# Six layers of local attention and gated feed-forward on one core: a new order for the weight loads at a change of layer

## The chip, the cores and the metric

The kernel runs on one core of one Trainium2 chip. The metric is the device time of one execution in microseconds (us). An execution is one launch that computes the whole output from inputs in device memory.

## The reference, cut to what matters

The input x is 32 sequences of 128 tokens of 128 values. A cross attention of 16 small heads (4 key heads) is added to it, and the result x1 is normalized. Then six layers run, each with its own weights, and x1 is added to what comes out:

```python
def shift_tokens(t):                      # 2nd half of the features comes from the token before
    a, s = split(t, 2, -1); s = pad(s, one token in front)[:, :-1]
    return concatenate([a, s], -1)
for i in range(6):
    x = attn_layer(shift_tokens(x), Wqkv[i], q_scale[i], k_scale[i], Wo[i]) + x
    x = ffn_layer(shift_tokens(x), ln_g[i], ln_b[i], W1[i], b1[i], W2[i], b2[i]) + x
```

`attn_layer` computes q, k and v with one 128 x 3072 matrix (16 heads of 64), normalizes q and k, rotates them with a table, attends in windows of 32 tokens (each window sees itself and the one before), and multiplies by the 1024 x 128 matrix Wo. `ffn_layer` is a layer norm with scale and bias, a product with W1 (128 x 682), a * gelu(gate), and a product with W2 (341 x 128) plus b2. Everything is in float32.

## The kernel before, in words

**Units and slots.** A unit is one sequence in one layer, so there are 6 x 32 = 192 units; unit u belongs to layer u // 32. All engines run the same list of slots (`slots`, L241), and a slot n works on several units at once, each at another stage: unit n is projected to q, k and v, unit n-2 is transposed and its scores are made, unit n-3 attends, unit n-4 goes through Wo, the second token shift, the layer norm and the product with W1, and unit n-5 through W2. A unit so takes six slots. Slots 6 to 189 are in a loop with two slots in its body, in which semaphore targets are computed from the loop's register; the slots before and after it are written out with constants. There is one buffer for each of the layer's weights, so a weight of the next layer can be loaded only once the last unit of the old layer has used it, and it must be there when the first unit of the new layer, one slot later, comes to it. This happens five times, at each change of layer.

**Order of the work in a slot.** TensorE (function `slot` in the tensor block) runs: attn_out (L1355), ffn_out, proj_qk(1), transpose_qk, transpose_z, proj_qk(2), proj_qk(3), transpose_P, scores, attend, transpose_zn, proj_v(0) (L1255), ffn_gate (L1385), ffn_a, proj_qk(0) of the next unit, proj_v(1). proj_qk(0) and (1) make the queries, (2) and (3) the keys, each from 512 columns of `wqkv`. VectorE runs z_mid (L996: attention output plus residual into `zm`) in the middle of its list, later norm_stats (L1005: statistics of the shifted row), which waits for the shift's transfer, and norm_apply (L1030), whose result transpose_zn waits for. GpSimd's last work of a slot is residual (L542), which adds b2 and raises `g_zmb`.

**The sync engine.** One queue, that of the sync engine, issues every transfer, in an order written out by hand from L385 on. A transfer is issued when the waits ahead of it are over, and whatever is written behind it waits too. For each unit there are two steps: shift_z(u) (L353) waits for z_mid of unit u and moves 127 rows of 256 bytes one partition down (the token shift of the feed-forward); shift_v(u) (L343) waits for the copies of v and for attend of unit u-2, and issues six copies of v rows. In a slot shift_z comes first and shift_v about 7 us ahead of the next shift_z. Between them, at a change of layer, stand the loads: load_qk (L289: 1 MB of query and key columns, waits for the last proj_qk, and then the rotary table `rot`, waits for the last rotary), load_v (L297), load_o (L302, waits for attn_out of the last unit), load_b2 (L338, waits for `g_zmb` of the last unit), load_w1 (L326), load_w2 (L331) and load_small (L319: layer-norm scale and bias and b1, from SBUF).

With `start` the first unit of a layer and `end` that of the next, the steps before a change stand in this order, the loads of the new layer in brackets: shift_z(end-5), [q and k, rot], shift_v(end-2), [v], shift_z(end-4), shift_v(end-1), shift_z(end-3), shift_v(end), shift_z(end-2), shift_v(end+1), [Wo], shift_z(end-1), [b2], shift_v(end+2), [W1], then shift_z(end), which is the new layer's shift_z(start), [small], [W2], shift_v(end+3).

Of the kernel before, what the change touches and what calls it, by code (L numbers as in the profile page):

```python
# [31 lines left out]
INNER = HEADS * DH  # L32
# [45 lines left out]
def build(nc, x, ctx, deltas, mask, xWq, xWk, xWv, xWo, xtw, Wqkv, qs, ks, Wo, lng, lnb, W1, b1, W2, b2, consts, out):  # L78
    es = ExitStack()
    with es:  # L80
# [6 lines left out]
        def sem(name):  # L87
# [94 lines left out]

        names = [

            "l_cst", "l_x", "l_x0", "l_xw", "l_dm", "l_ctx0", "l_ctx1", "l_qks", "l_wqk", "l_wv", "l_wo", "l_w1", "l_w2",
            "l_gb", "l_small", "u_small", "l_b2", "l_rot", "l_v0", "l_v1", "l_s0", "l_s1", "u_s0",
            "u_bf", "u_ones", "u_wkr", "u_rotq", "u_dmT", "u_dmc", "u_ct", "u_ctc", "u_st", "u_ag", "u_ve", "u_rstd", "u_nmr",
            "u_negh", "u_vz", "u_v1", "u_zs",
# [26 lines left out]
        def wait(eng, name, value):  # L215

            if not (isinstance(value, int) and value <= 0):
                eng.wait_ge(s[name], value)
# [54 lines left out]
        def _(sp):  # L273
# [12 lines left out]
                sp.dma_start(zv[:, 8 * c:8 * c + 8, :], xr[:, 8 * c:8 * c + 8, :]).then_inc(s["l_x"], 16)  # L286


            def load_qk(layer):  # L289
                w = Wqkv[layer, :, :]  # L290
                wait(sp, "p_qk", 4 * B * layer)
                sp.dma_start(wqkv[:, 0:2 * INNER], w[:, 0:2 * INNER]).then_inc(s["l_wqk"], 16)
                if layer > 0:
                    wait(sp, "d_rot", 4 * B * layer)
                    sp.dma_start(rot[:, :], rot_all[:, layer, :]).then_inc(s["l_rot"], 16)

            def load_v(layer):  # L297
                w = Wqkv[layer, :, :]
# [20 lines left out]
            def load_small(layer):  # L319

                wait(sp, "a_gelu", B * layer)
                wait(sp, "d_h", B * layer)
                sp.wait_ge(s["l_small"], 128)
                sp.dma_start(small[:, :], small_all[:, layer, :]).then_inc(s["l_gb"], 16)
# [6 lines left out]
            def load_w2(layer):  # L331

                wait(sp, "p_y2", B * layer)
                sp.dma_start(w2[:, 0:2, :], W2[layer, 0:256, :].rearrange("(c p) n -> p c n", p=128))\
                    .then_inc(s["l_w2"], 16)
                sp.dma_start(w2[0:FF - 256, 2, :], W2[layer, 256:FF, :]).then_inc(s["l_w2"], 16)
# [16 lines left out]
            def shift_z(u, par):  # L353

                wait(sp, "d_zm", count(1, u, 1))
                sp.dma_start(zm[1:128, par, 1, :], zm[0:127, par, 2, :]).then_inc(s[f"l_s{par}"], 16)
# [2 lines left out]
            sp.dma_start(qks[:, 1, :], ks.rearrange("l d -> (l d)").partition_broadcast(128)).then_inc(s["l_qks"], 16)  # L359


            load_qk(0)
            load_v(0)
            load_o(0)
            load_b2(0)
# [19 lines left out]
            for layer in range(DEPTH):  # L385

                start, end = B * layer, B * layer + B
                if layer == 0:
                    for u in range(3):
                        shift_v(u, u % 2)  # L390
                shift_z(start, 0)
                if layer > 0:
                    load_small(layer)
                    load_w2(layer)
                shift_v(start + 3, 1)
                shift_z(start + 1, 1)
                shift_v(start + 4, 0)
                with sp.Fori(0, (B - 8) // 2) as i:
                    for k in range(2):
                        shift_z(i * 2 + (start + 2 + k), k)  # L400
                        shift_v(i * 2 + (start + 5 + k), (3 + k) % 2)
                shift_z(end - 6, 0)
                shift_v(end - 3, 1)
                shift_z(end - 5, 1)
                if layer + 1 < DEPTH:
                    load_qk(layer + 1)
                shift_v(end - 2, 0)
                if layer + 1 < DEPTH:
                    load_v(layer + 1)
                shift_z(end - 4, 0)  # L410
                shift_v(end - 1, 1)
                shift_z(end - 3, 1)
                if layer + 1 < DEPTH:
                    shift_v(end, 0)
                shift_z(end - 2, 0)
                if layer + 1 < DEPTH:
                    shift_v(end + 1, 1)
                    load_o(layer + 1)
                if layer + 1 == DEPTH:
                    store(0, 6)  # L420
                shift_z(end - 1, 1)
                if layer + 1 < DEPTH:
                    load_b2(layer + 1)
                    shift_v(end + 2, 0)
                    load_w1(layer + 1)
            store(6, 9)
            sp.wait_ge(s["out_done"], 144)

# [695 lines left out]
        def _(pe):  # L1124
# [104 lines left out]
            def slot(n, k):  # L1229
# [9 lines left out]
                def proj_qk(j):  # L1239

                    u, u_on, pu = (zu, z_on, (k + 1) % 2) if j == 0 else (a, a_on, k % 2)
                    if u_on:
                        if j == 0:
                            if isinstance(u, int) and u == 0:
                                pe.wait_ge(s["x_add"], 4 * B)
                            wait(pe, "a_zs", count(2, u, 2))
                            wait(pe, "l_wqk", 16 * layer_of(u) + 16)
                        if j < 2:
                            wait(pe, "a_v", count(2, u - 1, j + 1))
                        else:  # L1250
                            wait(pe, "d_rot", count(4, u, j - 1))
                        t_.matmul(bank[j % 2][:, :], zsT[:, pu, :], wqkv[:, 512 * j:512 * j + 512],  # L1252
                                  start=True, stop=True).then_inc(s["p_qk"], 1)
# [193 lines left out]
```

## Time and profile before

| | us |
|---|---|
| median of 3 runs | 3308.8 |
| lowest and highest run | 3306.87 and 3309.24 |
| span of the profiled execution | 3304.7 |
| busy TensorE, VectorE, ScalarE, GpSimd (share) | 3125.4 (95%), 2884.0 (87%), 2663.4 (81%), 2447.9 (74%) |
| slots of a layer without a change | 15.0 each |

The span runs from the first to the last instruction of the profiled execution. That execution's own time is not listed beside its span; the three runs lie 2.2 to 4.5 us above the span, and that is what lies around it. All times of rows are us from the start of the span. L12 is line 12 of the kernel before.

### The profile page before, as it was taken

What the parts mean: (1) busy time and instruction counts of PE and PEld (TensorE: products, weight loads), DVE (VectorE), ACT (ScalarE), POOL (GpSimd) and SP (SyncE); (2) the same over time, 40 slices, a digit from 0 to 9 for tenths busy, and PEclk for the clock granted to TensorE, in tenths of its full rate; (3) what the DMA queues carried; (4) which work ended last, traced back from release to release, by engine and by line L of the source; (5) the groups of instructions that cost most, each with busy time, mean ns of one, the idle gap of its engine ahead of it and who ended that gap; (6) DMA issues with size and microseconds to landing.
All of it is one profiled execution on the core that took longest, in us unless ns stands there. A gap on an engine that the chain in (4) does not pass through costs nothing.

```text
span 3304.7 us, 181505 instructions
## 1 busy us (share of the span) xinstructions
PE 3125.4 (95%) x71268; PEld 2192.5 (66%) x71268; DVE 2884.0 (87%) x6045; ACT 2663.4 (81%) x5440; POOL 2447.9 (74%) x2673
## 2 busy tenths in 40 slices
PE   6776899999999999999999999999999999999996
PEld 4443567676667676676767667676676767667665
DVE  7886789999899999899999899998899999899984
ACT  6886678888788888788888788888788888788874
POOL 3333778888788888788888778787787878788883
PEclk9988999999999999999999999999999999999997
DMA  3000112122222222222222212122221212212121
GB/s 79 8 7 10 47 51 59 50 59 71 67 56 53 56 53 77 63 54 55 54 55 74 68 50 59 50 59 77 57 59 50 59 50 77 66 50 59 50 58 50
DMA packets 150374, 182.24 MB, mean 55 GB/s; under 512 B 51572, under 2 KB 74162, under 8 KB 149554
## 3 DMA queue, kind: packets, MB, share of 16 engines
q1 hardware_dynamic: 150322, 181.55, 21.2%
q8 instruction: 33, 0.54, 0.1%
q14 instruction: 19, 0.16, 0.0%
HBM read 21.32 MB, written 2.10 MB: 7 GB/s over the span
## 4 chain that ended last, share of the span: by engine, by line
PE 57%; issue 13%; DVE 10%; ACT 10%; POOL 5%; SPq 1%; DVEq 1%; DMA 1%; ACTq 1%; POOLq 0%
PE bank L1252 13%; PE bank L1339 8%; PE bank L1322 7%; PE bank L1262 5%; PE bank L1363 5%; PE bank L1270 3%; PE bank L1290 3%; ACT L798 3%; DVE tb L966 3%; ACT P L774 3%; PE bank L1392 2%; ACT gl L766 2%; POOL qk L524 2%; DVE bank L1075 2%; PE bank L1400 2%
## 5 line engine op out<-in xcount | busy, mean ns | idle before, releaser
L533 POOL TENSOR_TENSOR qk<-qk,rn 128x512 f32<-128x512 f32 x768 | 803.0, 1046 | 356.8 <-DVE rn L985 356.8
L524 POOL TENSOR_TENSOR qk<-ta,tb 128x512 f32<-128x512 f32 x768 | 978.6, 1274 | 2.5 <-DVE tb L966 2.5
L1252 PE MATMUL bank<-wqkv,zsT 128*128 128x512 f32 x1536 | 819.9, 617 | 25.4 <-ACT vt L705 12.3
L963 DVE TENSOR_TENSOR ta<-bank,rot 128x512 f32<-128x512 f32 x768 | 527.5, 687 | 116.1 <-ACT sq L688 87.4
L966 DVE TENSOR_TENSOR tb<-bank,rot 128x512 f32<-128x512 f32 x768 | 523.0, 681 | 0.0
L1068 DVE TENSOR_REDUCE bank<-sq 128x32 f32<-128x2048 f32 x192 | 440.6, 2295 | 25.1
L688 ACT ACTIVATE sq<-bank 128x512 f32<-128x512 f32 x768 | 445.2, 611 | 14.8 <-PE bank L1252 12.1
L696 ACT ACTIVATE qkT<-bank 128x512 f32<-128x512 f32 x768 | 396.6, 602 | 57.1 <-PE bank L1290 56.9
L1363 PEld LDWEIGHTS bank<-wo,oT 128*128 128x128 f32 x3072 | 375.4, 193 | 92.4 <-issue 92.4
L743 ACT ACTIVATE znT<-bank,small 128x128 f32<-128x128 f32 x192 | 87.9, 458 | 431.8 <-PE bank L1383 431.8
L564 POOL TENSOR_TENSOR P<-P,rowsum 128x512 f32<-128x512 f32 x384 | 392.9, 1045 | 20.0 <-DVE rowsum L1083 20.0
L1262 PE MATMUL bank<-wqkv,zsT 128*128 128x512 f32 x768 | 399.8, 603 | 1.2 <-DVE tb L966 1.1
L1363 PE MATMUL bank<-wo,oT 128*128 128x128 f32 x3072 | 376.6, 276 | 0.5 <-ACT gl L766 0.5
L1252 PEld LDWEIGHTS bank<-wqkv,zsT 128*128 128x128 f32 x1536 | 238.0, 195 | 193.1 <-DVE tb L966 170.2
L1290 PEld LDWEIGHTS bank<-cst,qk 32*128 32x128 f32 x12288 | 212.5, 137 | 172.9 <-issue 172.9
L1339 PE MATMUL bank<-PT,vs 64*64 64x32 f32 (+1 forms) x18432 | 310.9, 220 | 11.3 <-issue 11.3
L1339 PEld LDWEIGHTS bank<-PT,vs 64*64 64x64 f32 x18432 | 291.4, 135 | 30.0 <-issue 12.3
L539 POOL TENSOR_TENSOR rstd<-ve,half_neg 128x1 f32<-128x1 f32 x192 | 105.8, 551 | 254.5 <-DVE ve L1023 254.5
L1075 DVE TENSOR_REDUCE bank<-P 128x16 f32<-128x1024 f32 x192 | 235.8, 1228 | 66.7 <-ACT P L774 66.6
L1322 PEld LDWEIGHTS bank<-qkT 64*32 64x32 f32 x24576 | 278.1, 105 | 14.1 <-issue 3.9
L1322 PE MATMUL bank<-qkT 64*32 64x64 f32 x24576 | 281.7, 225 | 3.0 <-issue 3.0
L1290 PE MATMUL bank<-cst,qk 32*128 32x32 f32 x12288 | 228.5, 223 | 21.0 <-DVE rowsum L1083 2.9
(131 smaller groups left out, 5740.6 us busy)
## 6 DMA issues: line engine op xcount, KB each, us to landing
vs<-vt SPq DMA_DIRECT2D x1152, 128.0 KB, 2.4
wqkv<-L_ffn_Wqkv SPq DMA_DIRECT2D x6, 1024.0 KB, 5.0
zm<-zm SPq DMA_DIRECT2D x192, 31.8 KB
wqkv<-L_ffn_Wqkv SPq DMA_DIRECT2D x6, 512.0 KB, 3.7
wo<-L_ffn_Wo SPq DMA_DIRECT2D x6, 512.0 KB, 4.0
z_sb<-x SPq DMA_DIRECT2D x4, 512.0 KB, 5.1
ctxb<-ctx SPq DMA_DIRECT2D x32, 64.0 KB, 1.8
w<-L_ffn_W SPq DMA_DIRECT2D x6, 341.0 KB
```

The source lines that it names most:

```text
L524: g.tensor_tensor(o, i0, i1, ALU.add).then_inc(s["g_add"], 1)
L533: g.tensor_tensor(q3, q3, r3, ALU.mult).then_inc(s["g_qk"], 1)
L688: a_.activation(sq[:, 512 * j:512 * j + 512], bank[j % 2][:, :], ACT.Square)\
L963: v_.tensor_tensor(ta[:, c].rearrange("p (h d) -> p h d", d=DH), bank[j % 2][:, :].rearrange("p (h d) -> p h d", d=DH), rot[:, o:o + 64].u ...
L966: v_.tensor_tensor(tb[:, c].rearrange("p (h c d) -> p h c d", c=2, d=32)[:, :, ::-1, :], bank[j % 2][:, :].rearrange("p (h c d) -> p h c d ...
L1068: v_.tensor_reduce(sm, sq[:, :].rearrange("p (h d) -> p h d", d=DH), AX.X, ALU.add)\
L1252: t_.matmul(bank[j % 2][:, :], zsT[:, pu, :], wqkv[:, 512 * j:512 * j + 512], start=True, stop=True).then_inc(s["p_qk"], 1)
L1262: t_.matmul(bank[r][:, :], zsT[:, k % 2, :], wv[:, :, r, :], start=True, stop=True)\
L1290: ins = t_.transpose(TB[t][:, 32 * p:32 * p + 32], qk[tok, pb, 128 * p:128 * p + 128], ident[tok, tok])
L1322: ins = t_.matmul(SC[e][32 * w:32 * w + 32, 64 * p:64 * p + 64], qkT[dr, p, 32 * w:32 * w + 32], qkT[dr, PAIRS + p, k0:k0 + 64], start=Fal ...
L1339: ins = t_.matmul(bank[4 + r][64 * e:64 * e + 64, 128 * i + q0:128 * i + q0 + nq], vs[kr, pc, w, hc:hc + 64], PT[kr, 4 * e + i, q0:q0 + nq ...
L1363: ins = t_.matmul(bank[7][:, 384:512], oT[:, p, :], wo[:, 2 * (p % 4) + p // 4, :], start=p == 0, stop=p == PAIRS - 1)
```

## The change

Four loads change their place in the sync engine's list, and one is split. W1 moves from ahead of shift_z(start) to behind it and behind `small`. b2, whose wait stood ahead of shift_v(end+2), stands behind it. Wo moves from ahead of shift_z(end-1) to behind it. v moves behind shift_z(end-4), and the rotary table behind shift_v(end-2). The 1 MB of query and key columns become two transfers of 512 KB with a semaphore each; the one for the queries waits for proj_qk(1) of the last unit and the one for the keys for proj_qk(3). On TensorE the wait for the weights at proj_qk(0) becomes one for the queries' columns, and proj_qk(2) has one for the keys' columns. The same holds in the prologue, where the first layer's columns are loaded in two transfers. The new order is: shift_z(end-5), [q], [k], shift_v(end-2), [rot], shift_z(end-4), [v], shift_v(end-1), shift_z(end-3), shift_v(end), shift_z(end-2), shift_v(end+1), shift_z(end-1), [Wo], shift_v(end+2), [b2], shift_z(start), [small], [W1], [W2], shift_v(start+3).

```diff
-            def load_qk(layer):
-                w = Wqkv[layer, :, :]
-                wait(sp, "p_qk", 4 * B * layer)
-                sp.dma_start(wqkv[:, 0:2 * INNER], w[:, 0:2 * INNER]).then_inc(s["l_wqk"], 16)
-                if layer > 0:
-                    wait(sp, "d_rot", 4 * B * layer)
-                    sp.dma_start(rot[:, :], rot_all[:, layer, :]).then_inc(s["l_rot"], 16)
+            def load_qk(layer, j):
+                wait(sp, "p_qk", 4 * B * layer - 2 + 2 * j if layer > 0 else 0)
+                c = slice(INNER * j, INNER * j + INNER)
+                sp.dma_start(wqkv[:, c], Wqkv[layer, :, c]).then_inc(s[("l_wq", "l_wk")[j]], 16)
+
+            def load_rot(layer):
+
+                wait(sp, "d_rot", 4 * B * layer)
+                sp.dma_start(rot[:, :], rot_all[:, layer, :]).then_inc(s["l_rot"], 16)
...
                 shift_z(start, 0)
                 if layer > 0:
                     load_small(layer)
+                    load_w1(layer)
                     load_w2(layer)
...
-                if layer + 1 < DEPTH:
-                    load_qk(layer + 1)
+                if not last:
+                    load_qk(layer + 1, 0)
+                    load_qk(layer + 1, 1)
                 shift_v(end - 2, 0)
-                if layer + 1 < DEPTH:
+                if not last:
+                    load_rot(layer + 1)
+                shift_z(end - 4, 0)
+                if not last:
                     load_v(layer + 1)
-                shift_z(end - 4, 0)
                 shift_v(end - 1, 1)
...
-                if layer + 1 < DEPTH:
+                if not last:
                     shift_v(end + 1, 1)
-                    load_o(layer + 1)
-                if layer + 1 == DEPTH:
+                else:
                     store(0, 6)
                 shift_z(end - 1, 1)
-                if layer + 1 < DEPTH:
+                if not last:
+                    load_o(layer + 1)
+                    shift_v(end + 2, 0)
                     load_b2(layer + 1)
-                    shift_v(end + 2, 0)
-                    load_w1(layer + 1)
...
                             wait(pe, "a_zs", count(2, u, 2))
-                            wait(pe, "l_wqk", 16 * layer_of(u) + 16)
+                        if j % 2 == 0:
+                            wait(pe, ("l_wq", "l_wk")[j // 2], 16 * layer_of(u) + 16)
```

## Rows read from the trace of the kernel before

**Rows 1.** The page: busy time, share of the span and instructions of each engine
```profile
PE 3125.4 (95%) x71268; PEld 2192.5 (66%) x71268; DVE 2884.0 (87%) x6045; ACT 2663.4 (81%) x5440; POOL 2447.9 (74%) x2673
```

**Rows 2.** Busy by stretch: length, engines' busy time, granted clock, DMA share, GB/s
```profile
860.00:880.00 20.00, 16.05 (x359) 11.85 (x358) 14.80 (x33) 13.61 (x26) 13.18 (x15) 0.91 0.42 110
898.00:1318.00 420.00, 415.84 (x10077) 295.07 (x10077) 381.46 (x781) 351.79 (x700) 341.28 (x364) 1.00 0.23 59
```

**Rows 3.** Shifts issued in a stretch: nanoseconds min/median/max, first to last start
```profile
L356 SPq DMA_DIRECT2D zm<-zm x133: 636/642/667, 832.4 to 2846.5; - x133
...
L356 SPq DMA_DIRECT2D zm<-zm x5: 637/652/661, 832.4 to 897.9; - x5
...
L356 SPq DMA_DIRECT2D zm<-zm x29: 640/642/661, 897.9 to 1318.8; - x29
```

**Rows 4.** VectorE's timeline: start, length, line, [idle before it, releaser]
```profile
851.78 0.30 DVE L1009 BATCH_NORM_STATS2 stats<-zm 128x6 f32<-128x128 f32 x1 [1.21 <-DMA zm<-zm]
...
862.35 0.29 DVE L1001 TENSOR_TENSOR zm<-bank,z_sb 128x128 f32<-128x128 f32 x1
...
870.76 0.29 DVE L1009 BATCH_NORM_STATS2 stats<-zm 128x6 f32<-128x128 f32 x1 [4.70 <-DMA zm<-zm]
```

**Rows 5.** TensorE's timeline, same columns: one stalled pair, one pair in step
```profile
804.04 0.33 PE L1377 MATMUL bank<-cst,zcur 128*128 128x128 f32 x1
804.20 2.29 PE L1252 MATMUL bank<-wqkv,zsT 128*128 128x512 f32 x4
...
810.40 1.02 PE L1262 MATMUL bank<-wqkv,zsT 128*128 128x512 f32 x2
811.28 0.93 PE L1392 MATMUL bank<-znT,w 128*128 128x128 f32 x6
...
874.48 0.33 PE L1383 MATMUL bank<-cst,zn 128*128 128x128 f32 x1 [3.57 <-DVE zn L1030]
874.69 1.37 PE L1262 MATMUL bank<-wqkv,zsT 128*128 128x512 f32 x2
```

**Rows 6.** Sync engine's timeline around the first change of layer
```profile
795.34 3.66 SPq L351 DMA_DIRECT2D vs<-vt  x6
...
802.33 0.65 SPq L356 DMA_DIRECT2D zm<-zm  x1
...
846.47 0.39 SPq L305 DMA_DIRECT2D wo<-L_ffn_Wo  x1
847.45 0.66 SPq L356 DMA_DIRECT2D zm<-zm  x1
861.71 0.34 SPq L341 DMA_DIRECT2D b2r<-L_ffn_b  x1
...
865.90 0.58 SPq L329 DMA_DIRECT2D w<-L_ffn_W  x1
866.53 0.65 SPq L356 DMA_DIRECT2D zm<-zm  x1
867.29 1.42 SPq L324 DMA_DIRECT2D small<-small_all  x1
```

**Rows 7.** Waits of the sync engine: total us, times, longest
```profile
SPq L341 <- POOL zmb L548: 67.6, 5, 13.6
```

**Rows 8.** Busy by stretch, columns of rows 2, while only a shift moves
```profile
833.00:835.50 2.50, 2.43 (x68) 1.55 (x68) 2.50 (x5) 2.24 (x5) 2.50 (x3) 1.00 0.06 13
```

**Rows 9.** Output weights (L305), all six issues: time from issue to landing
```profile
DMA to landing us min/median/max: 3.9/4.0/9.0
```

**Rows 10.** Rotary table (L295), its five issues: time from issue to landing
```profile
DMA to landing us min/median/max: 2.3/2.4/3.1
```

**Rows 11.** VectorE's timeline: first use of the new layer's rotary table
```profile
802.83 0.69 DVE L963 TENSOR_TENSOR ta<-bank,rot 128x512 f32<-128x512 f32 x1 [0.17 <-issue]
```

**Rows 12.** Prologue: the sync engine's and TensorE's timeline
```profile
10.96 0.43 SPq L292 DMA_DIRECT2D wqkv<-L_ffn_Wqkv  x1
...
30.31 0.48 PE L1195 MATMUL bank<-cst,ctxb 128*128 128x128 f32 x1 [2.13 <-DMA ctxb<-ctx]
```

More of the change, by code:

```diff
@@ L183, in build @@
         names = [
-            "l_cst", "l_x", "l_x0", "l_xw", "l_dm", "l_ctx0", "l_ctx1", "l_qks", "l_wqk", "l_wv", "l_wo", "l_w1", "l_w2",
+            "l_cst", "l_x", "l_x0", "l_xw", "l_dm", "l_ctx0", "l_ctx1", "l_qks", "l_wq", "l_wk", "l_wv", "l_wo", "l_w1", "l_w2",
             "l_gb", "l_small", "u_small", "l_b2", "l_rot", "l_v0", "l_v1", "l_s0", "l_s1", "u_s0",
@@ L359, in _ @@
             sp.dma_start(qks[:, 1, :], ks.rearrange("l d -> (l d)").partition_broadcast(128)).then_inc(s["l_qks"], 16)
-            load_qk(0)
+            for j in range(2):
+                load_qk(0, j)
             load_v(0)
@@ L387, in _ @@
                 start, end = B * layer, B * layer + B
+                last = layer + 1 == DEPTH
                 if layer == 0:
@@ L404, in _ @@
                 shift_z(end - 5, 1)
-                if layer + 1 < DEPTH:
-                    load_qk(layer + 1)
+                if not last:
+                    load_qk(layer + 1, 0)
+                    load_qk(layer + 1, 1)
                 shift_v(end - 2, 0)
-                if layer + 1 < DEPTH:
+                if not last:
+                    load_rot(layer + 1)
+                shift_z(end - 4, 0)
+                if not last:
                     load_v(layer + 1)
-                shift_z(end - 4, 0)
                 shift_v(end - 1, 1)
                 shift_z(end - 3, 1)
-                if layer + 1 < DEPTH:
+                if not last:
                     shift_v(end, 0)
                 shift_z(end - 2, 0)
-                if layer + 1 < DEPTH:
+                if not last:
                     shift_v(end + 1, 1)
-                    load_o(layer + 1)
-                if layer + 1 == DEPTH:
+                else:
                     store(0, 6)
                 shift_z(end - 1, 1)
-                if layer + 1 < DEPTH:
+                if not last:
+                    load_o(layer + 1)
+                    shift_v(end + 2, 0)
                     load_b2(layer + 1)
-                    shift_v(end + 2, 0)
-                    load_w1(layer + 1)
             store(6, 9)
```

## The prediction

> **What bounds the kernel now.** The page comes first: TensorE is busy for 95% of the span, VectorE for 87% [rows 1]. That is an average, so the second view is the busy time by stretch. Over 420 us inside a layer TensorE is busy for 415.84, or 99%, at a granted clock of 1.00; over the 20 us around the first change of layer it is busy for 16.05, or 80%, and the granted clock is 0.91 [rows 2]. Inside a layer TensorE is the bound, at a change it is not. How much the changes cost is read from the token shifts, one per slot. Inside a layer 29 of them are issued between 897.9 and 1318.8, so a slot lasts 420.9 / 28 = 15.03 us. From the slots before the first change to those behind the fifth, 133 are issued between 832.4 and 2846.5: 132 slots in 2014.1 us, where 132 x 15.03 would be 1984.2 [rows 3]. The five changes so cost 29.9 us together, 6.0 each; the first costs 65.5 - 4 x 15.03 = 5.4.
>
> Where it goes is read on VectorE and TensorE. In the new layer's first slot VectorE has z_mid done at 862.35 + 0.29 = 862.64, and then norm_stats, at 870.76, has waited 4.70 us for the shift's transfer [rows 4]. TensorE stands for 3.57 us in front of transpose_zn, which needs the normalized rows, and the projections behind it take 1.37 us where they take 1.02 in a slot in step [rows 5]. That is the lower clock of the stretch [rows 2]: 1.2 GHz instead of 2.4 for a part of it, granted after TensorE had stood idle.
>
> Why the shift is late is read on the sync engine. Its input is ready at 862.64, but it is issued at 866.53 [rows 6], 3.9 us late. Ahead of it in the queue stands load_b2, whose wait for GpSimd's residual of the last unit takes 67.6 us in 5 times, up to 13.6 at once [rows 7], and ends at 861.71. Only then come the six copies of shift_v (3.66 us in all, by the same step at 795.34) and W1 at 865.90 [rows 6]. So the copies of v, which nobody needs for a slot, are held back by b2, and they hold back the shift, which VectorE needs at once.
>
> **The change part by part.** *b2 behind the copies, W1 behind the shift.* shift_v(end+2) is no longer held. In a slot in step the copies begin 802.33 - 795.34 = 7.0 us ahead of the next shift [rows 6], so here at 862.7 - 7.0 = 855.7, and they are out by 859.4. b2 still goes out at 861.71 with its 0.34 us, and the queue is free at 862.05, 0.6 us before z_mid ends. Shift_z(start) goes at 862.7 instead of 866.53. It then lands at the latest as slowly as the two shifts which have a weight right ahead of them: W1 at 865.90 ahead of 866.53, with the statistics at 870.76, 4.2 us after the issue, and Wo at 846.47 ahead of 847.45, with the statistics at 851.78, 4.3 us after [rows 4, 6]. So the statistics start by 867.0. Left of the 4.70 us is at most 0.9. What that costs is seen at 851.78: an idle of 1.21 us there, and the next z_mid ends 862.64 - 847.45 = 15.2 us after the issue of that shift, 0.2 longer than a slot [rows 3, 4, 6]. The whole excess goes, -29.9, the clock's part of it as well because TensorE no longer stands; and I leave 0.2 per change, +1.0, for b2, which is now the transfer right ahead of the shift.
>
> *W1, small and W2 behind the shift.* `small` goes at 863.4 and takes 1.42 us of the queue [rows 6], W1 goes at 864.9, W2 at 865.5, all is out by 866.5 and the next copies come at 870.7. In a slot in step ffn_gate, the first reader of W1, starts 811.28 - 802.33 = 8.95 us after the shift [rows 5, 6], so here at 871.6. W1's own landing is not in the trace; the nearest rows are the output weights, which are larger: 4.0 us as a rule and 9.0 at worst, in the crowded prologue [rows 9]. With 4.0 it is there at 868.9 and costs nothing. W2, b2 and Wo are needed still later, by the end of the slot or in the next. Wo, now issued at 848.1 behind its shift, lands at 852.1 and has until attn_out in the next slot, shortly before the z_mid of 862.35 [rows 4]; its shift loses the transfer ahead of it, a part of the -29.9.
>
> *The other shifts that get a weight behind them.* These are shift_z(end-5) with q, shift_z(end-4) with v and shift_z(end-1) with Wo. What a transfer does that is issued behind a shift, no row shows by itself. A shift uses one sixteenth of the transfer engines' time while it moves alone, a share of 0.06 [rows 8], so a large transfer behind it shares one of sixteen engines with it and has to let it pass there. I take nothing, with 0.2 for each as for a weight ahead as the other end: 0 to 3 x 5 x 0.2 = 3.0. The Trainium skill, "DMA: Bandwidth & Descriptors", section "Why a DMA increments its semaphore by 16 and not by 1", says that 127 partitions put a whole transfer on a single engine, and its section on queues that an engine takes descriptors in ring order; by that rule the shift loses nothing to what is behind it, the transfer behind loses up to the shift's time, and the 0.06 of the row agrees.
>
> *q and k in two.* q goes a few us earlier than the 1 MB did and k when that did, and each is smaller; nothing in the new order makes either later, so 0. The additional issue of about 0.4 us falls into time in which the queue waits. *The rotary table* now follows six copies: 795.34 + 3.66 = 799.05, landing 2.3 to 3.1 us later [rows 6, 10], 801.4 to 802.1. VectorE's first use is at 802.83 [rows 11]. This is the narrowest cover of the change, 0.7 us; were the table behind the copies by 1 us more than its slowest landing, it would cost 0.3 x 5 = 2. I take 0. *v* goes at 803.0 behind shift_z(end-4), lands at 807.0 with the 4.0 of Wo, and is read by proj_v(0) at 810.40 [rows 5, 9]: 0.
>
> *Prologue.* One more issue, 0.43 us and a gap of 0.05 [rows 12]. The queue is at work all the way to the context tiles, and TensorE stands 2.13 us for one of them at 30.31 [rows 12]. So this one is on the path: +0.5, between 0 and 0.5.
>
> *The new wait on TensorE* for the keys' columns stands in every slot, 184 of them with computed targets, in front of proj_qk(2), on the engine that is the bound. Behind it is queued all of TensorE's slot. The nearest rows are two places where a single transpose is followed by a projection after two such waits. At 874.48 the queue had just run dry, so each wait shows: the projection follows 0.21 us later. At 804.04, in step, the projection behind transpose_z follows 0.16 us later [rows 5]. Two waits in the open so cost 0.05 us, and one in front of proj_qk(2) costs between 0 and 0.05: 0 to 184 x 0.05 = 9.2. I take 0: in step one wait already stands between transpose_z and proj_qk(2), and the 0.16 show no trace of it, because ahead of both are the 64 pairs of transpose_qk, during which the waits can be worked off. The Trainium skill, "TensorE: Matmul & The Clock Gate", section "Architectural detail: the array is 16× 32×32, not 1× 128×128", gives TensorE a queue of 64 instructions; by that the sequencer is far enough ahead and the wait costs nothing, without it the sum would be up to 9.2 worse. The trace agrees as far as 0.16 against 0.21 goes.
>
> **Sum:** -29.9 + 1.0 + 0.5 = -28.4. The profiled execution's span would be 3304.7 - 28.4 = 3276.3. The median lies 4.1 above the span, within the 2.2 to 4.5 of the runs, and I keep that distance: 3308.8 - 28.4 = 3280.4.
>
> **The rivals.** *A, the new wait is seen.* Its price is up to 0.05 us per slot: up to 3280.4 + 9.2 = 3289.6. For it speaks that TensorE is 99% busy, against it the step of 0.16. *B, slower than before:* the same wait at its worst. If both waits and the matmul behind them needed the whole 0.21 us in the open at proj_qk(2), with nothing hidden, the result is 3280.4 + 184 x 0.21 = 3319.0. It decides from 28.4 / 184 = 0.154 us per slot. Against it: the 0.16 in step, with one such wait inside. *C, a weight comes late:* with the 9.0 of the prologue W1 lands at 864.9 + 9.0 = 873.9, 2.3 after 871.6, times five is 11: 3292. Should W1's part on the shift's engine only begin when the shift has landed (867.0), it lands at 871.0 with the 4.0, still in time by 0.6. *D, the shift was not what bound the slot:* only the 3.57 us in which TensorE stands come back, and another wait keeps the rest: 5 x 3.57 = 17.9, so 3308.8 - 17.9 + 1.5 = 3292.4. Against it: nothing else in that slot stands for long. *E, the shift is not issued earlier,* because b2's wait, now directly ahead of it, ends later than z_mid: 3308.8 or close to it. The 0.6 us between 862.05 and 862.64 speak against it.
>
> **How the numbers follow.** The forecast has 0.76, A 0.09, C 0.05, D 0.04, E and smaller mixtures of losses that end near the old time 0.04, B 0.02. The range starts at 3308.8 - 29.9, less the 2.4 by which the runs shown differ, 3276.5, and reaches to 3280.4 + 9.2 + 3.0 = 3292.6, rounded to 3293, which takes in A, C and D. A measurement of this kernel can tell about 0.2%, 6.6 us, from no change. Beyond that lie the forecast, A, C and D: faster 0.94; same 0.04; slower 0.02.
>
> **What would show it.** In the changed kernel's trace: each new layer's first shift issued within 0.1 us of z_mid; norm_stats idle for less than 1.3 us there instead of 4.70; no TensorE wait of 3.57; a granted clock of 1.00 over the changes; 132 slots in about 1985; no wait of proj_qk, proj_v, ffn_gate or rotary for a transfer. The forecast is wrong if slots inside a layer last longer than 15.03 (A, B), if TensorE or ScalarE waits for `w1` or `small` (C), or if the slots of a change stay above 15.3 with the shift in time (D).

## The result and the profile after

The changed kernel takes 3270.95 us (median of 4 runs, 3270.27 to 3273.11), the kernel before beside it 3308.12 (4 runs, 3306.87 to 3309.24): a ratio of 0.9891, with an interval of 0.9877 to 0.9905. The forecast was faster, 3280.4 in a range of 3276.5 to 3293.0. The direction holds, and so does the mechanism at the changes of layer, but the time lies 9.5 us below the forecast and 5.6 us below the range. The profiled execution took 3271.08 with a span of 3269.0, against 3304.7: 35.7 us less.

First the shifts, as in [rows 3]: the first row is all 192 of the kernel before, the second all 192 of the changed kernel, the third the same 133 around the five changes as in the first of [rows 3]. Line numbers in a run's rows are those of its own kernel.

```profile
L356 SPq DMA_DIRECT2D zm<-zm x192: 626/642/682, 375.4 to 3290.0; - x192
```

```profile
L358 SPq DMA_DIRECT2D zm<-zm x192: 633/642/682, 371.5 to 3255.0; - x192
...
L358 SPq DMA_DIRECT2D zm<-zm x133: 637/642/664, 828.7 to 2812.1; - x133
```

The 132 slots around the changes last 2812.1 - 828.7 = 1983.4 us instead of 2014.1. That is 30.7 us less, and it is what 132 slots of 15.03 last without any change of layer. The other 5.0 us of this pair of traces are elsewhere: the first shift comes 3.9 us earlier, and the remaining stretches (the rest of layer 0 and of the last layer, and the end) give 1.1. So 31 of the 36 us are the mechanism of the prediction, and 5 are not in it.

The sync engine at the first change, to be held against [rows 6]:

```profile
795.42 0.59 SPq L297 DMA_DIRECT2D rot<-rot_all  x1
798.68 0.65 SPq L358 DMA_DIRECT2D zm<-zm  x1
799.37 0.84 SPq L302 DMA_DIRECT2D wqkv<-L_ffn_Wqkv  x1
...
843.77 0.64 SPq L358 DMA_DIRECT2D zm<-zm  x1
844.45 0.87 SPq L307 DMA_DIRECT2D wo<-L_ffn_Wo  x1
851.77 3.68 SPq L353 DMA_DIRECT2D vs<-vt  x6
857.54 0.35 SPq L343 DMA_DIRECT2D b2r<-L_ffn_b  x1
858.76 0.66 SPq L358 DMA_DIRECT2D zm<-zm  x1
859.53 0.80 SPq L326 DMA_DIRECT2D small<-small_all  x1
860.38 0.60 SPq L331 DMA_DIRECT2D w<-L_ffn_W  x1
```

The six copies now go out 8 us behind the shift of 843.77, as in any slot; b2 follows when GpSimd is done, and the new layer's first shift goes at 858.76, 0.31 us after z_mid began. On VectorE (the rows answer to [rows 4]):

```profile
847.61 0.29 DVE L1016 BATCH_NORM_STATS2 stats<-zm 128x6 f32<-128x128 f32 x1 [0.73 <-DMA zm<-zm]
...
858.45 0.28 DVE L1008 TENSOR_TENSOR zm<-bank,z_sb 128x128 f32<-128x128 f32 x1
...
862.18 0.29 DVE L1016 BATCH_NORM_STATS2 stats<-zm 128x6 f32<-128x128 f32 x1 [0.23 <-DMA zm<-zm]
```

The wait of 4.70 is 0.23, and slots inside a layer have 0.21 to 0.30. The sync engine's wait for GpSimd ahead of b2, 67.6 us before [rows 7], is 11.0, and the shift behind it is in time. TensorE is busy through the change, at full clock; its rows by stretch are to be held against [rows 2] and those of the pair against [rows 5]:

```profile
898.00:1318.00 420.00, 416.11 (x10080) 295.19 (x10079) 381.57 (x785) 351.77 (x700) 340.57 (x364) 1.00 0.23 59
860.00:880.00 20.00, 19.79 (x552) 13.71 (x545) 17.83 (x38) 17.24 (x36) 16.07 (x18) 1.00 0.27 70
```

```profile
860.47 0.33 PE L1385 MATMUL bank<-cst,zcur 128*128 128x128 f32 x1
860.64 2.29 PE L1260 MATMUL bank<-wqkv,zsT 128*128 128x512 f32 x4
...
866.65 0.33 PE L1391 MATMUL bank<-cst,zn 128*128 128x128 f32 x1
866.82 1.02 PE L1270 MATMUL bank<-wqkv,zsT 128*128 128x512 f32 x2
```

From transpose_z to the keys' projection it is 0.17 us, with the new wait between them, where it was 0.16 without. No projection waits for a weight anywhere. The granted clock rises from 0.99 to 1.00 over the stretch from 800 to 2850. Over the first 372 us, where the slots are not in step, it is 0.90 in both kernels, so it does not explain why the first shift comes 3.9 us earlier (columns as in [rows 2]; the first fence is the kernel before, the second the changed one):

```profile
0.00:372.00 372.00, 271.95 (x2715) 160.10 (x2716) 289.48 (x720) 269.27 (x697) 141.20 (x212) 0.90 0.11 28
...
800.00:2850.00 2050.00, 2010.57 (x48328) 1427.13 (x48328) 1836.55 (x3767) 1695.70 (x3361) 1637.03 (x1747) 0.99 0.23 60
```

```profile
0.00:372.00 372.00, 270.25 (x2733) 161.31 (x2733) 290.31 (x726) 271.51 (x701) 141.15 (x213) 0.90 0.11 28
...
800.00:2850.00 2050.00, 2030.35 (x49244) 1439.66 (x49236) 1861.97 (x3821) 1716.77 (x3411) 1661.99 (x1775) 1.00 0.24 61
```

### The profile page after: what moved, and what is told of

Same layout as the page of the kernel before. It is cut to its first block, busy times and chain, and to the rows that moved or that the text cites. A ratio compares the mean times of both kernels' runs of the same rounds, so it can differ in the third digit from the quotient of the medians.

```text
span 3269.0 us, 181519 instructions
## 1 busy us (share of the span) xinstructions
PE 3107.6 (95%) x71268; PEld 2181.0 (67%) x71268; DVE 2881.0 (88%) x6045; ACT 2659.6 (81%) x5440; POOL 2446.6 (75%) x2673
## 4 chain that ended last, share of the span: by engine, by line
PE 60%; issue 12%; ACT 11%; DVE 10%; POOL 3%; DVEq 1%; SPq 1%; ACTq 1%; DMA 0%; POOLq 0%
PE bank L1260 14%; PE bank L1347 9%; PE bank L1330 7%; PE bank L1371 5%; PE bank L1270 5%; PE bank L1278 4%; ACT L805 4%; PE bank L1298 4%; DVE tb L973 3%; ACT P L781 3%; PE bank L1400 2%; ACT gl L773 2%; DVE bank L1082 2%; PE bank L1408 2%; PE bank L1322 2%
## 5 line engine op out<-in xcount | busy, mean ns | idle before, releaser
L1371 PEld LDWEIGHTS bank<-wo,oT 128*128 128x128 f32 x3072 | 375.2, 193 | 91.8 <-issue 91.8
L1371 PE MATMUL bank<-wo,oT 128*128 128x128 f32 x3072 | 376.6, 276 | 0.5 <-ACT gl L773 0.5
```

The source lines that it names most:

```text
L1371: ins = t_.matmul(bank[7][:, 384:512], oT[:, p, :], wo[:, 2 * (p % 4) + p // 4, :], start=p == 0, stop=p == PAIRS - 1)
```

## The experiments

The table puts the traces of the runs side by side; each number is read off the shifts as above. Times are medians; "before" is the kernel before on the same chip. "First shift" is where the layers begin, "132 slots" is the stretch around the five changes. The profiled execution is one of the runs, and not always the median one; a kernel has one trace, so a difference of a few us in the last two columns can be chance.

| run | us | before | ratio (interval) | first shift | 132 slots |
|---|---|---|---|---|---|
| changed kernel | 3270.95 | 3308.12 | 0.9891 (0.9877 to 0.9905) | 371.5 | 1983.4 |
| e5, changed again | 3270.83 | 3305.12 | 0.9899 (0.9884 to 0.9914) | 372.8 | 1983.1 |
| e1, b2 and W1 moved only | 3280.0 | 3307.24 | 0.9917 (0.9901 to 0.9934) | 376.6 | 1985.2 |
| e13, as e1 | 3279.08 | 3307.05 | 0.9915 (0.9902 to 0.9929) | 378.1 | 1985.3 |
| e6, b2 ahead again | 3292.58 | 3305.12 | 0.9964 (0.995 to 0.9977) | 375.2 | 2001.7 |
| e11, W1 ahead again | 3272.86 | 3305.61 | 0.9908 (0.9892 to 0.9925) | 374.1 | 1983.9 |
| e12, Wo ahead again | 3274.31 | 3305.61 | 0.9904 (0.9887 to 0.992) | 376.6 | 1984.2 |
| e7, one transfer, one wait | 3277.47 | 3305.12 | 0.9917 (0.9904 to 0.9931) | 372.3 | 1983.7 |
| e8, small loads behind context | 3271.42 | 3305.12 | 0.9902 (0.9887 to 0.9917) | 371.7 | 1983.0 |
| e2, second wait only | 3302.88 | 3307.24 | 0.9989 (0.9979 to 0.9999) | 377.0 | 2010.1 |
| e3, prologue only | 3307.01 | 3307.24 | 0.9999 (0.9989 to 1.0009) | 379.7 | 2013.0 |
| e4, split only | 3304.67 | 3307.24 | 0.999 (0.9981 to 1.0) | 378.7 | 2012.1 |

**First, the two moves that the prediction rests on, alone (e1).** In the kernel before:

```diff
-                    load_b2(layer + 1)
                     shift_v(end + 2, 0)
-                    load_w1(layer + 1)
+                    load_b2(layer + 1)
...
                     load_small(layer)
+                    load_w1(layer)
                     load_w2(layer)
```

> The kernel before with two of the moves alone: b2's load behind the copies of v, and W1's load behind the new layer's first token shift. Everything else (one transfer for queries and keys, rotary table, v and Wo where they were, the prologue, TensorE's waits) is that of before. Theory 1 (the changes of layer give back all of the 29.9 us, and a shorter prologue stage gives the rest): 3308 - 29 to 3308 - 31 = 3277 to 3279, first shift of the layers at 375.4 us as before. Theory 2 (all of the 37 us come from the late shift and its consequences): 3271, and the first shift of the layers early, near 371.5, or the slots inside a layer shorter than 15.03. Theory 3 (the moves of Wo, v and the rotary table carry a good part of it): above 3280, with slots of a change over 15.03.

3280.0 us, 27.2 below the kernel before on its chip, and 132 slots in 2818.5 - 833.3 = 1985.2:

```profile
L356 SPq DMA_DIRECT2D zm<-zm x133: 636/642/667, 833.3 to 2818.5; - x133
```

So 28.9 of the 30.7 us at the changes come from these two moves. The rest of the change gives 1.8 there. The time is 1 us above the range of theory 1, and theories 2 and 3 are out. But the changed kernel is some 9 us below e1, and of that only the 1.8 are at the changes.

**b2 ahead of the copies again, in the changed kernel (e6).**

```diff
-                    shift_v(end + 2, 0)
                     load_b2(layer + 1)
+                    shift_v(end + 2, 0)
```

> The changed kernel with b2's load put back ahead of the copies of v (b2, then the six copies, then the new layer's first shift, W1 still behind the shift). Theory 1 (b2's wait in front of the copies is the cause): the shift is issued when the copies are out, some 3.2 us late instead of 3.9, norm_stats waits about 3 to 4 us at each change, and most of the gain is gone: 3276 + 5 x 3 to 5 x 5 = 3291 to 3301. Theory 2 (W1's issue and traffic ahead of the shift was the main thing): within 5 us of the changed kernel.

3292.58, 21.8 us above e5 on the same chip. At the first change:

```profile
860.29 0.34 SPq L343 DMA_DIRECT2D b2r<-L_ffn_b  x1
860.74 3.67 SPq L353 DMA_DIRECT2D vs<-vt  x6
864.45 0.65 SPq L358 DMA_DIRECT2D zm<-zm  x1
```

```profile
868.01 0.29 DVE L1016 BATCH_NORM_STATS2 stats<-zm 128x6 f32<-128x128 f32 x1 [3.38 <-DMA zm<-zm]
```

```profile
871.73 0.38 PE L1391 MATMUL bank<-cst,zn 128*128 128x128 f32 x1 [2.32 <-DVE zn L1037]
871.90 1.95 PE L1270 MATMUL bank<-wqkv,zsT 128*128 128x512 f32 x2
```

The queue again stands for GpSimd in front of the copies, the shift comes late, VectorE waits 3.38 and TensorE 2.32 us, and the 132 slots take 2001.7, 18.6 more than in e5. Each change costs 3.6 to 3.7 us again. The place of b2's wait is the cause of these 18.6; theory 2 is out.

**W1 ahead of the shift again (e11) and Wo ahead of its shift again (e12).** e11 takes load_w1 out of its place behind load_small and puts it behind load_b2; e12 is

```diff
                     shift_v(end + 1, 1)
+                    load_o(layer + 1)
...
-                    load_o(layer + 1)
                     shift_v(end + 2, 0)
```

> The changed kernel with W1 issued again directly ahead of the new layer's first shift, behind b2 (b2 stays behind the copies). It is issued when b2 is out, about 0.9 us ahead of z_mid, so the shift itself is still in time. Theory 1 (a weight ahead of the shift costs what I read off the kernel before: the landing late by 0.9 us, a slot of 15.2 instead of 15.03): +0.2 x 5 = 1 us, 3272, norm_stats idle by about 1.2 us at each change. Theory 2 (W1 ahead delays the shift in full): 3 us and more per change, over 3285.

> The changed kernel with Wo issued again ahead of shift_z(end-1), as in the kernel before. Theory 1 (the moves of Wo, v and the rotary table are worth 1.7 us together by the traces of e1 and the changed kernel, and most of it is Wo, whose shift landed 1 us late in the kernel before): 0.2 to 0.3 us at each change, +1 to +1.5, 3272. Theory 2 (these moves carry the difference between 3280 of e1 and 3271): 3276 and more.

3272.86 and 3274.31, neither clearly apart from the changed kernel, which ran on two other chips. The 132 slots say more: 1983.9 and 1984.2 against 1983.1 and 1983.4, so 0.1 to 0.2 us for each change. In e11 the statistics of the new layer's first unit wait 1.08 us:

```profile
864.26 0.29 DVE L1016 BATCH_NORM_STATS2 stats<-zm 128x6 f32<-128x128 f32 x1 [1.08 <-DMA zm<-zm]
```

That is the 0.9 us later landing that [rows 4, 6] gave for a weight right ahead, and the slot absorbs nearly all of it. The row at 847.61 above shows the other side: with Wo right behind its shift instead of ahead, the statistics still wait 0.73 instead of 0.23. The other changes show the same. In slots without a load near the shift the statistics start 3.40 to 3.43 us after its issue, with Wo right behind it 3.84 to 4.11, with v right behind it 3.68 to 3.76, and with Wo right ahead of it, in the kernel before, 4.08 to 4.36. A large transfer that follows a shift directly is not free for it either; here it costs no slot time.

**The second wait on TensorE alone (e2), and the prologue's additional issue alone (e3).** e2 adds to the kernel before

```diff
                             wait(pe, "a_zs", count(2, u, 2))
+                        if j % 2 == 0:
                             wait(pe, "l_wqk", 16 * layer_of(u) + 16)
```

e3 loads only the first layer's query and key columns in two transfers.

> The kernel before with only one thing added: TensorE waits a second time in each slot for the query and key weights, in front of proj_qk(2), on the semaphore that it has waited for at proj_qk(0). Theory 1 (the wait is hidden behind the transposes): 3308 within 2 us, slots inside a layer 15.03. Theory 2 (it costs up to 0.05 us in each of 184 slots): up to 3317. Should it come out faster than before, the added instructions shift something else, such as where the low-clock stretches of the cross attention fall.

> The kernel before with only the first layer's query and key columns loaded in two transfers in the prologue (the semaphore's targets are 16 higher), so one more issue of 0.43 us ahead of the context tiles and nothing else. Theory 1 (the cross attention ends 3.9 us earlier in the changed kernel because its third context tile comes later and the low-clock stretches fall elsewhere): first shift of the layers near 371.5 instead of 375.4, time 3303 to 3306. Theory 2 (my prediction's term): +0.5, so 3308.5 and the first shift at 375.9. Theory 3 (the time of that stage differs from run to run by some us whatever the kernel): anything between 371 and 376, and the runs of one kernel spread as much.

e2 is faster than the kernel before by 4.4 us (10 runs against 25), its interval ends just below 1. The wait costs nothing that can be seen; it comes with a gain. e3 is no different from before (within some 3 us, so a term of 0.5 can't be seen in it), although its third context tile comes 2 us later than in [rows 12]:

```profile
32.36 0.48 PE L1196 MATMUL bank<-cst,ctxb 128*128 128x128 f32 x1 [4.21 <-DMA ctxb<-ctx]
```

In e3's one trace the first shift comes at 379.7, late by more than these 2 us, and its time is no longer for it. e8 is the test from the other side; it moves the small loads behind the third and fourth context tile:

```diff
-            load_all_small()
-            load_small(0)
             for b in range(2, B):
+                if b == 4:
+                    load_all_small()
+                    load_small(0)
```

> The changed kernel with one more move, in the prologue: the eight small layer-norm and bias loads and `small` itself (5.6 us and more of the queue, and a wait for their landing) stand behind the third and fourth context tile instead of ahead of them. TensorE waited 2.89 us for the third context tile in the changed kernel's trace. Theory 1 (that wait is on the path): 2 to 3 us below e5. Theory 2 (the low-clock stretches of the cross attention decide where that stage ends, not its start): anything within 4 us of e5 either way.

3271.42 against e5's 3270.83. TensorE starts on the third tile at 28.04 without a wait, 3.1 us earlier than in the changed kernel, and the layers begin at 371.7, where they begin at 371.5 and 372.8 in the two traces of the changed kernel. No gain can be seen: theory 2. When the cross attention gets its third tile does not decide when it ends.

**The split alone (e4).** The kernel before with two transfers, two semaphores and both waits, in the old order.

> The kernel before with query and key columns in two transfers with a semaphore each, in the prologue and at each change, and TensorE's two waits for them; the order of everything else as before. Theory 1: the sum of the second wait (0), of the prologue's additional issue (-3.9) and of the earlier queries (0): 3303 to 3306, changes of layer costing 6 us each as before. Theory 2 (the prediction's terms): 3308.5. Theory 3 (the smaller transfers also shorten the changes): under 3300, with the 132 slots around the five changes in less than 2012 us.

3304.67, 2.6 below before, with the upper end of its interval at 1.0. The 132 slots take 2012.1. That is no more than e2 has, so the transfers as such bring nothing that e2's wait does not.

**The changed kernel again (e5), and without split and second wait (e7).** e7 has one load_qk of 1 MB and `wait(pe, "l_wq", ...)` at proj_qk(0) alone.

> The changed kernel itself once more, on one chip with the three kernels below and with many runs of the kernel before. Its trace owes 30.7 us to the five changes, 3.7 us to what lies before layer 0 is in step and 1.3 us to the rest. Theory 1 (the 3.7 and 1.3 us are where low-clock stretches of the first and last stages happened to fall, which differs from run to run): 3307 - 31 = 3276 here, 3274 to 3278, its runs some us apart. Theory 2 (they belong to the change): 3270 to 3272 again.

> The changed kernel with queries and keys loaded in one transfer again and with one wait on TensorE (at proj_qk(0)) in place of two; b2, W1, Wo, v and the rotary table stay where the change put them. Theory 1 (split and second wait do nothing that can be measured once the changes are in step): as e5, within 2 us. Theory 2 (the second wait makes the kernel faster by the 4 us that e2 showed): 3 to 5 us above e5. Theory 3 (the wait costs up to 0.05 us per slot): up to 9 us below e5.

e5 repeats the time of the changed kernel to 0.1 us on another chip, with the kernel before at 3305.12, so the change brings 34.3 us there and 37.2 in the first comparison. e7 is 6.6 above e5: all eight runs of the changed kernel (both comparisons) lie at 3273.61 or below, and four of e7's five at 3276.19 or above. The slots around the changes are nearly as short in e7, 1983.7, so here the difference isn't made at the changes. Nor does its trace have it in one place: the layers begin at 372.3, as in e5, and the profiled executions are 3.7 us apart.

**Which wait, and where (e9, e10, e13 to e18).** e9 and e17 are e1 with e2's wait. e10 is the changed kernel with both waits at proj_qk(0). e13 is e1 again; on its chip e14 has `pe.nop()` in place of the wait, e15 the wait in the looped slots only and e16 in the written-out slots only. e18 is the changed kernel with a wait ahead of each of the four projections.

> The kernel of e1 (b2 behind the copies, W1 behind the shift, nothing else moved, one transfer for queries and keys) with the second wait of e2 on TensorE in front of proj_qk(2). e1 took 3280.0, e2 alone 4.4 us less than before, and the changed kernel without the second wait (e7) 6.6 us more than with it. Theory 1 (the second wait makes the kernel faster by 4 to 6 us wherever it stands, by the stages outside the steady slots): 3274 to 3276. Theory 2 (e2 and e7 were chance of runs that differ by some us): 3280. If theory 1 holds, the 132 slots around the changes stay at 1985 us and the gain lies ahead of the first shift, in the slots up to the fifth and behind the last change.

> The changed kernel with its two transfers and two semaphores, but with both waits at proj_qk(0) instead of one at proj_qk(0) and one at proj_qk(2). Theory 1 (it is the place of the second wait ahead of the keys' projection that brings 4 to 6 us): as e7, about 3277. Theory 2 (any additional wait does it, or the two transfers do): 3271. Theory 3 (nothing but chance): between the two, without a clear difference from either.

> The kernel of e1 unchanged, as the base of the three below, on one chip with them. Theory 1 (a kernel with one wait for queries and keys is 5 to 10 us slower than one with two): 3278 to 3281. Theory 2 (e1's 3280.0 was that chip's or that hour's): 3270 to 3274.

> The kernel of e1 with a no-operation on TensorE in front of proj_qk(2) in every slot, in place of e9's second wait. It computes no target and waits for nothing. Theory 1 (what helps is an instruction more in TensorE's list, whatever it is): as e9, 3270. Theory 2 (the computed target and the wait itself matter): as e13.

> The kernel of e1 with the second wait in the looped slots alone (184 of them), not in the slots written out. Theory 1 (the steady slots gain, 0.008 us each by the traces, 1.5 us in all): 1 to 2 us below e13, slots inside a layer 15.017 instead of 15.023. Theory 2 (the gain is made in the slots written out at either end): as e13.

> The kernel of e1 with the second wait only in the slots written out, the first six and the last ones. Theory 1 (the gain lies in the first slots or the last, where the length of TensorE's list or the moment of a low-clock stretch decides): as e9, 3270, that is 5 to 10 us below e13. Theory 2 (it is made in the loop): as e13.

> The kernel of e9 unchanged (b2 behind the copies, W1 behind the shift, second wait in every slot), on another chip. The wait in the loop alone brought 2.7 us and in the written-out slots alone 3.4 against e13's 3279.1. Theory 1 (both add up): 3273. Theory 2 (e9's 3269.6 is right and the two halves together bring more than their sum): 3270. Theory 3 (e9 was chance, the second wait does little): 3277 to 3279.

> The changed kernel with TensorE's wait for the weights in front of each of the four query and key projections instead of two of them. Theory 1 (every additional computed wait brings something, for a reason not yet found): below 3270, toward 3266. Theory 2 (only the step from one to two does, by where instructions or low-clock stretches fall): 3270 to 3273. Theory 3 (waits cost where they stand in the open, in front of proj_qk(1) and (3)): above 3274, slots inside a layer over 15.02.

| run | us | runs from, to | before | ratio (interval) |
|---|---|---|---|---|
| e9, e1 and second wait | 3269.64 | 3268.49, 3276.28 | 3305.61 | 0.9892 (0.9875 to 0.9908) |
| e17, the same | 3275.1 | 3273.08, 3278.22 | 3305.99 | 0.9906 (0.9892 to 0.9919) |
| e10, both at proj_qk(0) | 3268.35 | 3267.71, 3275.15 | 3305.61 | 0.9888 (0.9872 to 0.9905) |
| e13, e1 again | 3279.08 | 3277.34, 3281.29 | 3307.05 | 0.9915 (0.9902 to 0.9929) |
| e14, nop | 3277.33 | 3272.90, 3282.82 | 3307.05 | 0.9911 (0.9897 to 0.9925) |
| e15, wait in the loop | 3276.4 | 3272.87, 3277.20 | 3307.05 | 0.9903 (0.9888 to 0.9919) |
| e16, wait written out | 3275.72 | 3274.26, 3277.35 | 3307.05 | 0.9903 (0.9888 to 0.9918) |
| e18, four waits | 3273.05 | 3272.71, 3279.04 | 3305.99 | 0.9905 (0.9891 to 0.992) |

e13 repeats e1, so that is no matter of a chip. The place of the second wait shows no effect (e10), more than two bring nothing more (e18), and the loop and the written-out slots each go some way (2.7 and 3.4 us below e13, of the 4.0 that e17 has and the 9.4 that e9 has). A nop gives 1.8, which the spread of its runs covers. e9 and e17 are one kernel and 5.5 us apart, so a part of e9's distance was chance. Each kernel with a second wait lies below its partner without one: e2 under before by 4.4, e4 by 2.6, e9 and e17 under e1 and e13 by 4 to 10, e5 under e7 by 6.6. The intervals of most pairs overlap. What stands is the direction, with a size of some 3 to 7 us that isn't sure, and without a cause. The traces give no place for it either. The first shift comes at 378.3, 378.9 and 377.7 in e9, e10 and e17, which have the second wait, and at 372.3 in e7, which has not; the traces of e9 and e10 are each the longest of four runs. In e2 the 132 slots are 4.1 us shorter than in the kernel before, where e5 and e7 differ by 0.6 there; 1.6 of the 4.1 are in the fifth change, around which e2 has the higher granted clock of the two (see the next section). No version is clearly faster than the changed kernel: e10 and e9 lie 1 to 3 us below it, inside the spread of the runs.

## Why the prediction was right or wrong

**The bound and the place were right.** The 29.9 us read from 132 slots were the right sum to claim, and the trace gives 30.7 for it. The miss of 9.5 us adds up as 1.8 at the changes, 0.5 for the prologue, 5.0 outside the changes and 2.2 between span and median. The wait chain is shown by taking the parts back: b2's wait ahead of the copies alone costs 18.6 of them (e6), W1 ahead of the shift 0.5 to 0.8 (e11), Wo 0.8 to 1.1 (e12), and the two moves alone bring 28.9 (e1). With the standing gone the granted clock is back at 1.00. The five changes of the kernel before cost 5.4, 6.6, 5.1, 6.1 and 6.4 us, and this goes with the clock. Around the first two of them, 40 us of the trace:

```profile
855.00:895.00 40.00, 35.92 (x764) 25.69 (x758) 32.21 (x62) 29.40 (x58) 29.15 (x32) 0.96 0.27 70
1340.00:1380.00 40.00, 35.87 (x848) 25.75 (x831) 31.29 (x65) 27.10 (x54) 27.74 (x31) 0.91 0.22 58
```

The granted clock is 0.96 at the first and 0.91 at the second; the third is like the first, the fourth and fifth like the second. In e2 the first, third and fifth have 0.96 and cost 4.7 to 4.8, the others 0.91 and 6.2.

**"I leave 0.2 per change, +1.0, for b2"** was not there: the statistics wait 0.23 behind b2. With the excess itself 0.8 too small this is the 1.8.

**The rotary table, v, W1 and Wo** are all covered. Their landing times at the changes were near what I took: the rotary table 2.1 to 2.2 (taken 2.3 to 3.1), v 4.2 to 4.3 (4.0), Wo 4.9 as a rule (4.0), W1 3.3 (4.0). v and Wo land later than the 3.7 and 4.0 which they had in the kernel before, now that each is issued directly behind a shift. The 0.9 at Wo would fit a transfer that has to let the shift pass on one of sixteen engines; no run shows that by itself. The Trainium skill, "DMA: Bandwidth & Descriptors", section "Queues, rings and completion order", says that an engine takes descriptors in ring order. It does not say that what is behind costs the transfer ahead nothing; that was my step, and the 0.73 at 847.61 is against it: the shift lands 0.4 to 0.7 us later with Wo behind it. My other end, 0.2 per shift, was for slot time, and none of it shows.

**"So this one is on the path: +0.5"** (the prologue) has no support. e3 is the additional issue alone and makes 0.2 us less, within some 3 us; e8 takes the wait for the tile away, 3.1 us, and gains nothing.

**"One in front of proj_qk(2) costs between 0 and 0.05 ... I take 0"** is the step that failed. The 0 was right for the place: 0.17 against 0.16 between the two rows, and slots inside a layer of 15.02, show the wait hidden. The Trainium skill, "TensorE: Matmul & The Clock Gate", section "Architectural detail: the array is 16× 32×32, not 1× 128×128", gives TensorE a queue of 64; these rows agree with what I worked out from it. But I bounded the term from below by nothing, without a reason that excludes a gain. Alone it came out 4.4 us faster (e2), and without it the changed kernel is 6.6 slower (e7), at 3277.47 and so inside the range. e7 lacks the split as well, but e9 and e17 have the wait without the split and lie 4 to 10 us below their partners. By the times, this is the term that put the result under the range. The traces bear it out only in part: 3.9 of the 5.0 us outside the changes are the early first shift, at 371.5, and e7, without the wait, has it at 372.3.

The price of 0.05, and with it the upper end of rival A, rests on the single 0.21 us at 874.48 in [rows 5], and nothing on record repeats it. In e6, at the same place and after 2.32 us of standing, the projection follows 0.17 us behind the transpose (871.73 and 871.90), and 0.16 to 0.17 at its other four changes, as in step. At a granted clock of 0.50 the two are 0.27 apart where TensorE has not stood at all (changed kernel):

```profile
356.73 0.47 PE L1385 MATMUL bank<-cst,zcur 128*128 128x128 f32 x1
357.00 3.27 PE L1260 MATMUL bank<-wqkv,zsT 128*128 128x512 f32 x4
```

At the other four changes of the kernel before, where TensorE has stood for 3.6 to 3.8 us, they are 0.26 to 0.27 apart as well, with transposes of 0.47 to 0.48 us. So at either clock the waits show no price in the open, and what made the one 0.21 is open.

**The base.** I took the sum from the profiled execution to the median shown. All executions lie 2.0 to 2.2 us above their span, so the profiled one, with a span of 3304.7, was the run of 3306.87, the lowest, and not near the 3308.8 of the median. The 2.2 to 4.5 us said to lie around the span compare three executions with the span of one. The changed kernel's median lies 2.0 above the span of its trace, where I had kept 4.1. The lower end of the range allowed 2.4 us for the runs' spread, from three runs. 25 runs of the kernel before on one chip go from 3302.86 to 3312.69, 9.8 us.

In these 25 the mean granted clock of a run goes with its time: the five fastest (up to 3304.46) have 0.978 to 0.980, the five slowest (from 3310.41) 0.974 to 0.976. Between kernels whose changes of layer are repaired alike it says less (clocks are means over their runs): e5 with 0.983 takes 3270.8 and e9 with 0.983 3269.6, but nine kernels with 0.980 or 0.981 take from 3271.4 (e8) to 3280.0 (e1). An estimate of the size: a clock lower by 0.001 over 3270 us is 3.3 us of TensorE at full speed. In the 25 runs 0.006 of clock goes with 9.8 us, half of what this estimate would make of it. So the 3 to 7 us may be lower-clock time; that is argued and not shown. Where they lie, and what a kernel with one wait more does otherwise, is open. Moving the third context tile 2 us later or 3 us earlier (e3, e8) did not do it.

Rivals A to E are out. None of the five was on the side on which the result lay: all that I worked out were losses.

## What to carry to other kernels

In a queue written out by hand, look at each wait that stands ahead of work which was ready before it: here a load that nobody needed for a slot waited 13 us for GpSimd and held back the one transfer on the path, and two moves gave 29 of 36 us. Read what such a place costs as the length of all slots around it less the same number of slots in step, which holds the follow-up costs too, the lower clock among them. And a price read off one row should be looked for in the others: the 0.21 us at the first change, read as the cost of two waits, stood alone among five changes. Where a kernel has stages in which TensorE often stands, find out how far its runs lie apart before a range is set: 10 us here, more than every small term of the sum.

## What the runs showed of the hardware

An additional wait in TensorE's list, on the engine that is busy for 99% inside a layer, cost no time that can be seen and came with some 3 to 7 us less, for a reason that is open, where I had 0 to 9 us more. Two semaphore waits in front of a matmul add nothing to the 0.16 us between a transpose and a projection, even when the engine has just stood (0.16 to 0.17 in e6); at the lower clock the step is 0.26 to 0.27, with or without such standing. With a transfer of 512 KB directly behind a shift of 127 rows that shift lands 0.3 to 0.7 us later, and with one directly ahead of it 0.7 to 1.0. Wo, issued directly behind a shift, lands 0.9 us later itself. A start on the third tile of the cross attention 3 us earlier brought no earlier end of that stage (e8).
